# First cross-attention of a decoder kernel: VectorE takes all copies of K, Q and turned rows, ScalarE three of four copies of probabilities, and the order is rewritten

## The reference

```python
Q = query @ W_q.T + b_q          # (query = layernorm(x), key = value = ctx)
K = key @ W_k.T + b_k
V = value @ W_v.T + b_v
# 16 heads of 16 columns, 128 rows per sequence
qk = jnp.einsum('bhqd,bhkd->bhqk', Q, K) / sqrt(16)
attn = jax.nn.softmax(qk, axis=-1)
out = jnp.einsum('bhqk,bhkd->bqhd', attn, V)
x = x + out @ W_o.T + b_o
```

## Time and profile before

| | us |
|---|---|
| median of 3 runs (1296.21 to 1299.11) | 1298.37 |
| the profiled execution, device time | 1303.35 |
| its span, first to last instruction | 1301.6 |
| from the first `scores` of the stage (719.78) to the last (865.29) | 145.5 |
| from there to the first PE work of the expert stage (889.55) | 24.3 |

### The profile page before, as it was taken

One profiled execution on the slowest core, in us unless ns is written; L12 is line 12 of the kernel. 1 busy time (PEld: TensorE's weight loads), 2 busy tenths in 40 slices (PEclk: granted clock), 3 DMA queues, 4 the chain that ended last, 5 costly groups with the idle time before them and its releaser, 6 DMA issues. The chain is left out here.

```text
span 1301.6 us, 21160 instructions
## 1 busy us (share of the span) xinstructions
PE 1146.6 (88%) x6835; PEld 899.2 (69%) x6835; DVE 828.3 (64%) x1863; ACT 655.3 (50%) x1916; POOL 663.0 (51%) x705
## 2 busy tenths in 40 slices
PE   4999999999978999999988698876499999995984
PEld 3888888888866887887866476655266666664862
DVE  6888889888872666666665667753543333324795
ACT  2555555555533555555554687771122444224873
POOL 3276767667561224233353666651157556552664
PEclk9999999999998999999999889996599999997995
DMA  4002010020100000000020214104332223222001
GB/s 155 10 1 77 1 42 35 16 60 16 17 1 1 2 1 1 1 1 1 1 57 10 103 69 179 82 2 138 109 64 44 47 41 50 41 37 70 1 17 49
DMA packets 38078, 53.73 MB, mean 41 GB/s; under 512 B 8320, under 2 KB 32896, under 8 KB 36448
## 3 DMA queue, kind: packets, MB, share of 16 engines
q1 hardware_dynamic: 29248, 42.28, 10.1%
q0 software_dynamic: 8736, 10.25, 4.8%
HBM read 40.78 MB, written 11.74 MB: 40 GB/s over the span
## 5 line engine op out<-in xcount | busy, mean ns | idle before, releaser
L414 DVE SCALAR_TENSOR_TENSOR ssm_conv<-bank,conv_w,ssm_conv 128x508 f32<-128x508 f32 (+2 forms) x240 | 159.2, 727 | 9.1 <-ACT ssm_conv L350 9.1
L705 ACT ACTIVATE a_prob<-a_prob,a_neg_max 128x128 f32<-128x128 f32 x256 | 99.7, 391 | 122.7 <-DVE a_neg_max L751 122.7
L1475 PE MATMUL bank<-expert_raw,e_rows_t 128*128 x312 | 149.4, 603 | 1.3 <-ACT e_rows_t L1562 1.3
L303 PE MATMUL bank<-w_out,ssm_u 128*128 128x256 f32 x640 | 143.5, 382 | 0.0
L303 PEld LDWEIGHTS bank<-w_out,ssm_u 128*128 128x128 f32 x640 | 119.9, 190 | 17.9
L808 POOL TENSOR_TENSOR a_prob<-a_prob,a_inv 128x512 f32<-128x512 f32 x64 | 66.1, 1040 | 118.5 <-DVE a_inv L756 118.5
L1084 ACT ACTIVATE x_prob<-bank,x_neg_max 128x128 f32<-128x128 f32 x256 | 90.0, 392 | 36.2 <-DVE x_neg_max L1061 36.2
L1402 POOL DMA_INDIRECT x_rows<-e_y,e_index x39 | 62.8, 1611 | 76.6 <-ACT e_y L1590 72.9
L508 POOL TENSOR_TENSOR act_t_lo<-ssm_turned,act_t_hi 128x512 fp32r<-128x512 f32 x40 | 51.5, 1289 | 97.8 <-ACT ssm_turned L375 97.8
L1728 DVE COPY e_h_t<-bank 128x512 f32<-128x512 f32 x39 | 27.0, 692 | 105.3 <-PE bank L1484 105.3
L1000 POOL TENSOR_TENSOR x_prob<-x_prob,x_inv 128x512 f32<-128x512 f32 x64 | 66.0, 1039 | 52.3 <-DVE x_inv L1065 52.2
(11 more groups left out here) (329 smaller groups left out, 3013.1 us busy)
## 6 DMA issues: line engine op xcount, KB each, us to landing
expert_raw<-in_experts_laid SPq DMA_DIRECT2D x8, 1536.0 KB, 7.6
attn_raw<-in_attn_w_laid SPq DMA_DIRECT2D x4, 1024.0 KB, 7.5
w_in_raw<-in_L_attn_in_proj_w SPq DMA_DIRECT2D x5, 640.0 KB, 8.4
w_out<-in_L_attn_out_proj_w SPq DMA_DIRECT2D x5, 512.0 KB, 3.7
x_res<-in_x SPq DMA_DIRECT2D x4, 512.0 KB, 5.6
x_context<-in_ctx_t_laid SPq DMA_DIRECT2D x8, 256.0 KB, 3.2
z_rows<-cv SPq DMA_DIRECT2D x4, 512.0 KB, 2.9
x_rows<-x_res SPq DMA_DIRECT2D x4, 512.0 KB, 4.6
```

What stands on the lines that cost most here:

```text
L303: mm = pe.matmul(UWY[h][:, s * D:(s + 1) * D], u[:, g % 2, c, t:t + P], w_out[:, c, :], start=(c == 0), stop=(c == KI - 1))
L414: op = dve.scalar_tensor_tensor(out=acc, in0=xs, scalar=conv_w[:, c, TAPS - 1 - back:TAPS - back], in1=acc, op0=ALU.mult, op1=ALU.add)
L705: e = act.activation(prob[:, m % 4, i, :], prob[:, m % 4, i, :], ACT.Exp, bias=neg_max[:, m % 4, i:i + 1], accum_out=total[:, m % 4, i:i + 1])
L1475: mm = pe.matmul(bank[:, :], rows_t[:, t % 2, k, :], W[:, bass.ds(at + (column + k * FFN), FFN)], start=(k == 0), stop=(k == KD - 1))
```

## The change

DVE now makes both versions of K in one phase (four instructions), the copy of the turned rows and the copy of Q. ACT gives these up and takes the copies of probabilities of tile 3 too, so that DVE keeps only tile 2. Two semaphores and the column of the masked bias disappear. Both tables are rewritten, ten times finer, so the order changes on every engine. The early ticks of the pairs 0 and 1 stay, but what was ACT's there is now DVE's.

In the order of the changed kernel a pair in the middle of the stage reads:

- PE: scores 9, turn_probs 8.3, 8.2, turn_z 5, outputs 8, project_q 5, turn_probs 9.0, project_o 8, turn_probs 9.1; scores 10, turn_probs 9.3, 9.2, project_k 6, outputs 9, turn_probs 10.0, project_o 9, project_v 6, turn_probs 10.1; scores 11.
- ACT: exps 8.0, 8.1, 8.3, 8.2, copies of probabilities 8.1, 8.0, 8.3, exps 9.0 and so on.
- DVE: copy_v 5, maxima 9.0, 9.1, copy 8.2, copy_z 5, maxima 9.3, invert 9.0, copy_out 8, invert 9.1, maxima 9.2, copy_q 5, invert 9.3, add 8, invert 9.2, measure_next 3; maxima 10.0, 10.1, copy 9.2, maxima 10.3, invert 10.0, copy_k 6, copy_out 9, invert 10.1, maxima 10.2, invert 10.3, measure 7, add 9, invert 10.2, copy_v 6; maxima 11.0.
- POOL: share_out 9.0, 9.1, 9.3, 9.2, norm 6, share_out 10.0, 10.1, 10.3, 10.2, add_bias 5, invert_next 2, invert 7.

```diff
-BEAT = 52
+BEAT = 525
 BY_PAIR = {
-    "project_k": 75, "project_v": 115, "copy_v": 102, "measure": 0, "invert": 86, "norm": 98, "turn_z": 136, "copy_z": 127,
-    "project_q": 159, "copy_q": 155, "add_bias": 250, "measure_next": 392, "invert_next": 446, "copy_k": 58, "copy_k_odd": 85}
+    "project_k": 906, "project_v": 1173, "copy_v": 1268, "measure": 138, "invert": 0, "norm": 475, "turn_z": 1348,
+    "copy_z": 1466, "project_q": 1456, "copy_q": 1701, "add_bias": 2029, "measure_next": 3899, "invert_next": 5185,
+    "copy_k": 1006}
 BY_SEQ = {
-    "scores": (197,), "maxima": (183, 185, 207, 188), "exps": (198, 210, 217, 215), "turn_probs": (240, 241, 269, 272),
-    "invert_sums": (197, 205, 232, 227), "outputs": (286,), "share_out": (207, 213, 248, 244), "project_o": (317,),
-    "add": (295,), "copy_probs": (222, 245, 253, 256), "copy_out": (281,)}
-DVE_COPIES = (2, 3,)
+    "scores": (1722,), "maxima": (1820, 1844, 2136, 2002), "exps": (2117, 2129, 2202, 2176),
+    "turn_probs": (2043, 2235, 2356, 2318), "invert_sums": (2010, 2128, 2287, 2226), "outputs": (2490,),
+    "share_out": (1677, 1927, 2012, 1943), "project_o": (2664,), "add": (2798,), "copy_probs": (2452, 2390, 2486, 2553),
+    "copy_out": (2603,)}
+DVE_COPIES = (2,)
...
-                for k in range(KD):
-                    kc = dve.tensor_scalar(k_t[:, n % 2, 0, k, :], job_bank(n)[:, k * PT:(k + 1) * PT], bk[:, k:k + 1],
-                                           sel[:, 0:1], ALU.add, ALU.mult)
-                kc.then_inc(k_even, 1)
+                for par in range(2):
+                    for k in range(KD):
+                        kc = dve.tensor_scalar(k_t[:, n % 2, par, k, :], job_bank(n)[:, k * PT:(k + 1) * PT], bk[:, k:k + 1],
+                                               sel[:, par:par + 1], ALU.add, ALU.mult)
+                kc.then_inc(k_copied, 1)
+            elif phase == "copy_z":
+                dve.wait_ge(tr_ready, n + 1)
+                dve.tensor_copy(z_t[:, :, :], job_bank(n)[:, :].rearrange("p (k t) -> p k t", k=KD)).then_inc(zt_copied, 1)
+            elif phase == "copy_q":
...
+                    qc = dve.tensor_scalar(q_t[:, n % 2, k, :], job_bank(n)[:, k * PT:(k + 1) * PT], XHEAD ** -0.5, bq_scaled[:, k:k + 1],
+                                           ALU.mult, ALU.add)
+                qc.then_inc(q_copied, 1)
...
-            elif phase == "copy_k_odd":
...
-            elif phase == "copy_z":
...
-            elif phase == "copy_q":
...
-        "scalar": ("copy_k_odd", "copy_z", "copy_q", "exps", "copy_probs"),
-        "vector": ("selections", "measure", "copy_k", "copy_v", "maxima", "invert_sums", "copy_probs", "copy_out", "add", "measure_next"),
+        "scalar": ("exps", "copy_probs"),
+        "vector": ("selections", "measure", "copy_k", "copy_z", "copy_q", "copy_v", "maxima", "invert_sums", "copy_probs", "copy_out", "add", "measure_next"),
```

More of the change, by code:

```diff
@@ L901, in stage_cross_attention @@
     columns = sb(low, "columns", [P, 8, KD])
-    bq, bk, bq_scaled, bk_odd, sel = (columns[:, i, :] for i in range(5))
+    bq, bk, bq_scaled, sel = (columns[:, i, :] for i in range(4))
     neg_max, total, inv = (sb(low, name, [P, 2, TILES, 4]) for name in ("neg_max", "total", "inv"))
@@ L922, in stage_cross_attention @@
     bias_loaded, bv_loaded, bo_loaded = sem("bias_loaded"), sem("bv_loaded"), sem("bo_loaded")
-    k_even, bk_odd_ready = sem("k_even"), sem("bk_odd_ready")
     bq_ready, sel_ready, v_cleared = sem("bq_ready"), sem("sel_ready"), sem("v_cleared")
@@ L1029, in vector @@
                 dve.wait_ge(sel_ready, 1)
-                dve.tensor_scalar(bk_odd[:, :], bk[:, :], sel[:, 1:2], None, ALU.mult).then_inc(bk_odd_ready, 1)
                 dve.tensor_scalar(bq_scaled[:, :], bq[:, :], XHEAD ** -0.5, None, ALU.mult).then_inc(bq_ready, 1)
@@ L1038, in vector @@
                     dve.wait_ge(s_ready[TILES - 1], (n - 1) * PAIR)
+                for par in range(2):
[7 more added lines that the diff above has]
+            elif phase == "copy_q":
+                if n == 0:
+                    dve.wait_ge(bq_ready, 1)
+                dve.wait_ge(q_ready, n + 1)
+                if n >= 2:
+                    dve.wait_ge(s_ready[TILES - 1], (n - 1) * PAIR)
                 for k in range(KD):
-                    kc = dve.tensor_scalar(k_t[:, n % 2, 0, k, :], job_bank(n)[:, k * PT:(k + 1) * PT], bk[:, k:k + 1],
-                                           sel[:, 0:1], ALU.add, ALU.mult)
-                kc.then_inc(k_even, 1)
+                    qc = dve.tensor_scalar(q_t[:, n % 2, k, :], job_bank(n)[:, k * PT:(k + 1) * PT], XHEAD ** -0.5, bq_scaled[:, k:k + 1],
+                                           ALU.mult, ALU.add)
+                qc.then_inc(q_copied, 1)
             elif phase == "copy_probs" and r in DVE_COPIES:
@@ L1086, in scalar @@
                 e.then_inc(exp_ready[r], 1)
-            elif phase == "copy_k_odd":
-                if n == 0:
-                    act.wait_ge(bk_odd_ready, 1)
-                act.wait_ge(k_even, n + 1)
-                for k in range(KD):
-                    kc = act.activation(k_t[:, n % 2, 1, k, :], job_bank(n)[:, k * PT:(k + 1) * PT], ACT.Identity, bias=bk_odd[:, k:k + 1],
-                                        scale=sel[:, 1:2])
-                kc.then_inc(k_copied, 1)
-            elif phase == "copy_z":
-                act.wait_ge(tr_ready, n + 1)
-                act.activation(z_t[:, :, :], job_bank(n)[:, :].rearrange("p (k t) -> p k t", k=KD), ACT.Copy).then_inc(zt_copied, 1)
-            elif phase == "copy_q":
[L1099 to L1107, removed]
             elif phase == "copy_probs" and r not in DVE_COPIES:
```

## The result

The changed kernel takes 1287.65 us (median of 4 runs, 1285.99 to 1288.49) against 1298.74 of the kernel before: a ratio of 0.9915, 95% interval 0.9895 to 0.9935, or 11.1 us less. In a second series of runs it took 1285.97 against 1299.13 (ratio 0.9896, 0.9879 to 0.9912). Faster, then, by 11 to 13 us; the forecast was 8.6 to 9 us.

What follows compares the result with a forecast made beforehand. A chain of handoffs, no full engine, was taken to bound the cross-attention. Pairs -9.1, first beats +0.7, next beat -0.5, self-attention tail +0.3 gave -8.6; from the 1298.37 median, 1289.8, rounded to 1289.5, range 1282 to 1298.

Steps and rivals of the forecast that it cites:

- the walk through the new order: Cross-attention pair followed engine by engine in listed order: beats of 8.08 and 9.57, 17.7 us a pair against 19.2.
- the clock term: Six cross-attention pairs: the same 3 us lost to PE's lowered clock as before, ends 0 and 8.
- the last stretch: Last scores to the expert stage, 24.26 us: chain kept, so 0, ends -1 and +0.5.
- The bound: Cross-attention: no engine full, a chain of handoffs bounds; every second beat loses some 2.7 us to the copy_v and outputs knot.
- The owners: Copies moved between ACT and DVE: DVE +1.3 us busy a pair, to about 15.3; ACT -1.3, to 14.4.
- my second rival: PE stays at full clock in the cross-attention; the 3 us and 0.7 go: 1284.8, down to 1282; chance 0.18.
- the first two beats: Cross-attention's start, at 0.72 of the clock: longer links ahead of the exponentials cost +0.7 us, ends 0 and +2.
- The tail of the self-attention: DVE gets 4.8 us of copies for two pairs between mask additions, mostly absorbed: +0.3, ends -0.5 and +2.7.
- a rival had +2.4 more: DVE's tail work in the self-attention lands on its loop of mask, maxima and exponentials: 1292; chance 0.09.
- The beat behind the pairs: The beat of 856.63, after the six pairs, takes 8.15 instead of 8.66: -0.5 us.
- The slower rival: Clock at 0.84 in every cross-attention pair: 20.5 us a pair, six 123, total 1303; chance 0.09.
- DVE as the bound at 86%: DVE busy 15.3 of 17.7 us; handoffs 0.05 us dearer put a pair back at 19.2: 1297 to 1300; chance 0.09.

Runs made afterwards that it cites:

- one swap: Kernel before with maxima of tile 2 moved ahead of copy_v in DVE's order, work and owners unchanged: 1290.01 us, ratio 0.9938.
- both swaps: Kernel before with maxima of tile 2 ahead of copy_v and measure_next ahead of its beat's first maxima on DVE: 1288.85 us, ratio 0.9922.
- the kernel that was 25 us slower than the one before: Kernel before's old tables combined with the changed kernel's phases and owners of copies: 1323.66 us, ratio 1.0184.
- one variant: Changed kernel with DVE also copying the probabilities of tile 3, right ahead of tile 2: 1294.85 us, ratio 0.9961.

## Why the prediction was right, point by point

In short: the walk through the new order was right, the clock term was wrong, and part of the agreement in the total is luck. My sum of -8.6 was made on a profiled execution and set against a median. From span to span it was -15.1: the six pairs came out 3.3 us lower than I said, the last stretch 1.9 and the unchanged rest 1.5. Against that, the profiled execution before lay 4.6 above its median and that of the changed kernel 0.6, so the medians are only 11.1 apart, and nothing in my sum accounts for this.

**The bound.** That the chain of handoffs bounds the stage and not an engine's fill, and that its longest link is the wait of the last exponentials behind `copy_v` and `outputs`, is shown: one swap takes 0.83 us off a pair, both swaps 1.43 of the 1.57 that the change gains in all (19.21 to 17.64). I had counted 2.7 us of waits on ACT in that beat, of which the two swaps give back 1.4, since PE then waits for `copy_v` and what hangs on it.

**The walk.** Predicted beats 8.08 and 9.57, measured 8.19 and 9.45; a pair 17.65 against 17.64; the misses of 0.11 and 0.12 cancel. Exponentials at 2.19 and 2.29 after `scores`, measured 2.26 in the beat shown; PE waiting 0.7 for the copy of tile 2 and 0.6 for `copy_out`, measured 0.70 to 0.86 and 0.42. That PE waits 0.23 for `share_out` once a pair, where I had said that POOL decides nothing, is small. A Q copy, without a row before, was taken at 0.45 a step; two of them last 0.88 against 0.99 of two K copies, so the price without a row did no harm.

**The owners.** I costed the moved copies at +1.3 us for DVE and -1.3 for ACT a pair, and the windows show +1.2 and -1.0. I had written that the order decides, and the runs show how far: the move of the copies is not what pays. Old tables with two swaps and the old owners reach 17.78 a pair and 1288.85 us; the ratio of 0.9922 lies inside the interval of the changed kernel's first series (0.9895 to 0.9935) and just above that of the second (0.9879 to 0.9912). The owners matter only together with an order made for them: old owners in the new order 18.7, new owners in the old order about 24. So the change as a bundle is faster, and two swaps on DVE are enough for nearly all of it. What each of the other moves in the two tables gives in the changed kernel was not measured, but for `measure_next`.

The Trainium skill's remark that VectorE is the farther one from PSUM (page "VectorE: DVE Perf Modes", section Specifications) does not show as one clear advantage here: a turned-rows copy took 0.68 us on DVE against 0.60 on ACT, K copies 0.53 against 0.56, Q copies 0.48 against 0.49.

**The clock.** This is the term that was mis-sized. I took 3 us of loss in the six pairs; the changed kernel lost none in either profiled execution. (The loss before was 3.7, not 3: I had counted the first and the last pair as 19.2, and they are 18.56 and 19.15 at full clock.) No loss was the premise of my second rival, to which I gave 0.18: it wanted 106.2 for the pairs, and they took 105.85. Its other half, full clock in the first two beats, did not come (0.77). The measured time lies between the forecast and that rival.

I had argued from PE's idle pieces, and the traces bear that out only in part. In the kernel before and in the one with one swap, ten pairs have an idle piece of 1.46 to 1.53 us; six of them show a clock of 0.84 or 0.91, four are at full clock. The new owners in the old order, with a piece of 3.1, show 0.86 to 0.93. In the changed kernel no piece in the pairs is over 1.0 us, and no pair lost any clock; but neither did one with tile 3 on DVE (1.30 in every pair) or with the old owners in the new order (up to 1.36). So shorter pieces go with full clock in these traces; what tips the balance no run isolates.

**The tail of the self-attention.** I took +0.3 with ends of -0.5 and +2.7, and a rival had +2.4 more. At a like clock it is -0.3 to -0.6; over all traces of the table above it runs from -0.9 to +0.9. So DVE's 4.8 us of added work were absorbed, as I said, the rival did not come, and the sign of what is left hangs on the clock of one execution.

**The last stretch.** Taken as 0 with -1 as an end; it was -1.9. Of this 0.5 lies ahead of the first exponentials (`scores` at 1.15 us instead of 2.04) and 1.4 behind the last ones, where the kernel before ran its last `outputs` in 1.89 us instead of 1.08 and its last `project_o` in 1.66 instead of 1.13: clock again, in the main. **The first two beats** (+0.7, measured +0.5) were right by luck: I had put the longer links into both, but the first lasts 9.80 in all twelve traces of this document, old order or new (PE waits 5.7 to 6.6 us for GpSimd in it), and the second alone grew, from 8.78 to 9.32. The beat behind the pairs (-0.5, measured -0.5) was right.

**The slower rival**, a pair at a clock of 0.84 throughout, did not come. DVE as the bound at 86% did not either; but one more copy a beat on it costs 0.88 us a pair, as the kernel with tile 3 on DVE shows.

Splitting the K copies beats both kernels: 1282 to 1283 us.

## What to carry to other kernels

Where several in-order engines hand tiles round, look for the instruction that waits for something late while others that are ready stand behind it; moving a neighbour past it can be worth all that a new division of labour is. Put work that nobody waits for into the hole where its engine idles for the next input (ahead of the first maxima), not behind it. A walk through two beats with start-to-start distances from the trace, engine by engine in listed order, gave the period to 0.1 us; it must follow the waits through every in-order queue, as the kernel that was 25 us slower than the one before shows. And a sum made on one profiled execution belongs beside that execution: ask what it lost to the clock before subtracting it from a median.

## What the runs showed of the hardware

The same kernel spreads from run to run, in the main with the mean granted clock: ten runs of one variant went from 1289.84 us at 0.952 to 1298.19 at 0.947, and the kernel before took 1303.35 in its profiled execution at 0.943 where its median was 1298.74. The mean clock does not settle the time, though: the kernel with one swap took 1290.0 at 0.950 and 1295.5 at 0.951. A sum made against one profiled execution carries that much error before any step of it is wrong; the stretches that the change does not touch (here -1.5 us in the rest of the program, and 1.4 us in the start of the first `project_k`) show how much. Inside the pairs the traces are far tighter: the six pairs of the changed kernel agree to 0.01 us, and in two executions lasted 17.64 to 17.66.
